# A two-layer graph network on one core: layer 0 gathers its raw input, with the dense stage begun beside its last nine quads

## The reference

```
# layer 0
qk, v  = x @ Wqk + bqk, x @ Wv + bv
score  = clip(sum(qk[dst] * qk[src], -1) / sqrt(128), -5, 5)
attn   = segment_softmax(score, dst)
h      = segment_sum(attn * v[src], dst) @ Wo + bo + x
x      = layernorm(x + gamma * norm(h) + beta)
# layer 1, 8 heads of 16
n      = norm(x) * ln1_w
xl, xr = n @ lin_l_w.T + lin_l_b, n @ lin_r_w.T + lin_r_b
z      = leaky_relu(xl[src] + xr[dst] + edge_attr @ lin_edge_w.T, 0.2)
alpha  = segment_softmax(sum_per_head(z * att), dst)
y      = x + segment_sum(alpha * xl[src], dst) + attn_bias
y      = y + relu(norm(y) * ln2_w @ fc_w.T) @ proj_w.T
x      = layernorm(x + y)
```

## Time and profile before

| | before |
|---|---|
| median of 3 runs | 3092.32 us (3090.11 to 3101.77) |
| profiled execution | 3122.75 us |
| its span | 3120.9 us |
| mean granted clock of TensorE | 0.862 |
| PE, PEld busy | 2211.6 (71%), 1775.4 us (57%) |
| DVE, ACT, POOL busy | 1709.5 (55%), 652.8 (21%), 1767.4 us (57%) |
| DMA | 413.24 MB, mean 132 GB/s |

### The profile page before, as it was taken

How to read it: one execution, slowest core, us unless ns; L and a number is a source line. 1 busy time by engine, 2 the same in 40 slices (tenths; PEclk the granted TensorE clock), 3 DMA queues, 4 the chain that set the end, 5 groups by cost and what they waited for, 6 DMA issues and landing times. The chain is left out here.

```text
span 3120.9 us, 55922 instructions
## 1 busy us (share of the span) xinstructions
PE 2211.6 (71%) x15187; PEld 1775.4 (57%) x15187; DVE 1709.5 (55%) x7262; ACT 652.8 (21%) x1876; POOL 1767.4 (57%) x1751
## 2 busy tenths in 40 slices
PE   4666666666666666656378777777777777788879
PEld 3666666666666666644255555555555555565656
DVE  4444444444444444478245555555655566565766
ACT  0222222222222222235021111111111111111123
POOL 2666666666666666644656555555555565555312
PEclk8988888888888888877688888888998999988869
DMA  6555555555555555513454444444444444444301
GB/s 212 158 150 148 152 151 150 149 151 151 149 149 151 151 151 149 139 44 88 141 163 130 121 137 133 123 130 138 137 134 120 132 139 137 137 124 130 92 15 38
DMA packets 392325, 413.24 MB, mean 132 GB/s; under 512 B 61167, under 2 KB 336367, under 8 KB 385360
## 3 DMA queue, kind: packets, MB, share of 16 engines
q1 hardware_dynamic: 304992, 233.79, 25.4%
q0 software_dynamic: 66560, 163.68, 19.3%
q10 hardware_dynamic: 20592, 13.63, 1.4%
HBM read 393.41 MB, written 17.47 MB: 132 GB/s over the span
## 5 line engine op out<-in xcount | busy, mean ns | idle before, releaser
L832 POOL DMA_INDIRECT rows<-xl_tab,src_cols x832 | 848.1, 1019 | 592.8 <-DVE message L974 356.4
L260 POOL DMA_INDIRECT rows<-qkv_tab,src_cols x832 | 819.7, 985 | 501.8 <-remote 250.1
L307 PE MATMUL tile_sums<-gather,rows 128*128 128x128 f32 x1664 | 401.6, 329 | 413.8 <-issue 396.8
L339 DVE CUSTOM_DVE_ANT_0 product<-rows,q_dst 128x128 f32<-128x128 f32 x832 | 233.7, 281 | 654.3 <-remote 641.5
L307 PEld LDWEIGHTS tile_sums<-gather,rows 128*128 128x128 f32 x1664 | 307.0, 230 | 460.7 <-issue 454.0
L996 DVE SCALAR_TENSOR_TENSOR node_sums<-node_sums,shrunk,tile_sums 128x128 f32 x832 | 280.7, 337 | 316.5 <-remote 294.6
L309 PE MATMUL tile_sums<-gather,ones 128*128 128x128 f32 x1664 | 380.8, 316 | 0.0
L883 PEld LDWEIGHTS z_ps<-spread,window 128*128 128x128 f32 x1664 | 253.3, 220 | 203.9 <-issue 101.8
L930 PE MATMUL tile_sums<-onehot,message 128*128 128x128 f32 x1664 | 304.3, 323 | 79.9 <-issue 72.0
L348 DVE TENSOR_TENSOR node_sums<-node_sums,tile_sums 128x256 f32 x832 | 350.8, 422 | 4.7 <-PE tile_sums L309 1.6
L930 PEld LDWEIGHTS tile_sums<-onehot,message 128*128 128x128 f32 x1664 | 245.3, 218 | 143.6 <-issue 129.9
(11 more groups left out here) (153 smaller groups left out, 2532.8 us busy)
## 6 DMA issues: line engine op xcount, KB each, us to landing
window<-qkv_tab SPq DMA_DIRECT2D x832, 64.0 KB
attr<-in_attrT SPq DMA_DIRECT2D x52, 1024.0 KB
window<-xr_tab SPq DMA_DIRECT2D x832, 64.0 KB
rel_bc<-rel_rows SPq DMA_DIRECT2D x208, 128.0 KB
rel_bc<-rel_rows SPq DMA_DIRECT2D x52, 512.0 KB
rows<-qkv_tab,src_cols POOLq DMA_INDIRECT x832
rows<-xl_tab,src_cols POOLq DMA_INDIRECT x832
qkv_tab<-qkv ACTq DMA_DIRECT2D x13, 512.0 KB, 4.9
```

Of the source, the lines that this page charges most:

```text
L260: nc.gpsimd.indirect_dma_start(out=rows[:, q * QT + i, :], out_offset=None, in_=qkv_tab, in_offset=bass.IndirectOffsetOnAxis(ap=src_cols[: ...
L307: nc.tensor.matmul(bank[:, i % 2, 0, :], rows[:, q * QT + i, P:], gather1[:, q % 2, i, :], start=True, stop=True)
L832: nc.gpsimd.indirect_dma_start(out=rows[:, r, i, :], out_offset=None, in_=xl_tab, in_offset=bass.IndirectOffsetOnAxis(ap=src_cols[:, tile: ...
```

## The change

Blocks (a) to (d) become one block, with all quads written out (no hardware loop), and its steps run from T = 0 to 217, with no barrier between layer 0 and the dense stage.

- The score of an edge is x[src] . (M x[dst] + m) + (m' x[dst] + c) up to scale, with M = Wqk Wqk^T. PE makes M and the vectors at the start from transposed weights, and from them a table `p_tab` of 129 columns per node (the last is the constant). The gathers read the input x itself (512 B a row), and wait only for `src_cols`, which is now loaded first. Four blocks of `p_tab` are made ahead and one in each of steps 0 to 8; SP's windows (129 wide) of quad Q < 13 wait for a stored block. Wv Wo is one matrix `w_vo`, applied in the dense stage.
- The weighted one-hot is not a transpose any more: ACT makes |column - rel| (`measure`, four Abs to bf16), the exponential and its negative, and Relu(weight - weight |column - rel|) (`weigh`, four). PE has 8 spread records a quad, in halves that wait for `scored` of the quad before, and 16 of `add_up`, one step later than before. DVE's sums are two quads behind as before. `node_sums` is cleared by block.
- The dense block b starts at step T = 199 + b: projection, residual and moments at T, root, shift and norm 0 at T+1, POOL's `add_parts` (three operations), moments 1 at T+4, root 1 and the transposes at T+5, tables at T+6, scaled by the reciprocal root, with centred weights `w_cen`, so that no norm of x1 is made there. POOL puts `add_parts` of blocks 0 to 3 behind the gathers of quads 204 to 207. Only four buffers of x (`x_nm`) are loaded, the first four 16 quads ahead.
- Layer 1: `AHEAD` is 4. The biases of lin_l and lin_r are the bias operands of ACT's two halves of z, roots and shifts for all x1 are made at the start, and ACT normalises x1 (`norm_x1`, four operations) at quads 9 to 21. Some semaphores are merged. The MLP block loads `lin_l_b` and adds it on POOL to the attention bias.

```diff
-    qkv_tab = nc.dram_tensor("qkv_tab", (NP, 2 * P), F32).ap()
+    p_tab = nc.dram_tensor("p_tab", (NP, P + 1), F32).ap()
+    AHEAD0 = 4
+    DENSE = 199
+    EARLY = 4
...
+        steps = max(quads + 2, DENSE + blocks + 6)
...
+                pool.wait_ge(src_in, DMA)
+                for Q in range(quads):
+                    r = Q % AHEAD0
+                    if Q >= AHEAD0:
+                        pool.wait_ge(summed, 2 * (Q - AHEAD0 + 1))
+                    for i in range(QT):
+                        tile = Q * QT + i
+                        nc.gpsimd.indirect_dma_start(
+                            out=rows[:, r, i, :], out_offset=None, in_=t["x"],
...
+                    if Q == quads - EARLY:
+                        pool.wait_ge(lr_loaded, 5 * DMA)
+                        pool.wait_ge(w_scaled, 1)
+                    if Q >= quads - EARLY:
+                        add_parts(Q - quads + EARLY)
+                for b in range(EARLY, blocks):
+                    add_parts(b)
...
+                for T in range(steps):
+                    for k in range(2):
+                        if T + 1 < quads:
+                            spread_p(T + 1, k)
+                        if 0 <= T - 1 < quads:
+                            add_up(T - 1, k)
+                    if T + QUADS < node_groups:
+                        make_p(T + QUADS)
+                    b = T - DENSE
...
+                    if 0 <= b < blocks:
+                        project(b)
...
+                    if 0 <= b - 6 < blocks:
+                        tables(b - 6)
+                    if 0 <= b - 5 < blocks:
+                        turn_y(b - 5)
...
+                for T in range(steps):
+                    if T < quads:
+                        measure(T)
...
+                    if 0 <= b - 1 < blocks:
+                        root0(b - 1)
+                    if 0 <= b - 5 < blocks:
+                        root1(b - 5)
+                    if T < quads:
+                        weigh(T)
+                    if 0 <= b - 1 < blocks:
+                        norm0(b - 1)
+                    if 0 <= b - 6 < blocks:
+                        keep_tables(b - 6)
+                    if 0 <= b - 5 < blocks:
+                        keep_hT(b - 5)
...
-    AHEAD = 8
+    AHEAD = 4
```

More of the change, by code:

```diff
@@ new lines, in build @@
+        xlr = sb("xlr", [P, 2, QT, 2 * P])
+        share = sb("share", [P, QT])
+        stats = sb("stats", [P, 2, QT, 6])
+        mv0 = sb("mv0", [P, 2, QT, 2])
+        std = sb("std", [P, 2, 2, QT])
+        rstd = sb("rstd", [P, 2, 2, QT])
+        shift = sb("shift", [P, 2, 2, QT])
+        p_dst = [ps(f"p_dst{i}", [P, 2, 2 * P]) for i in range(2)]
+        tile_sums = [ps(f"tile_sums{i}", [P, 2, 2, P]) for i in range(2)]
+        o_ps = ps("o_ps", [P, QT, P])
+        t_ps = ps("t_ps", [P, QT, P])
@@ new lines, in build @@
+        lr_loaded = sem("l01_weights_in")
+        w_flipped = sem("w_flipped")
+        w_kept = sem("w_kept")
+        m_made = sem("m_made")
+        m_kept = sem("m_kept")
+        x_in = [sem(f"xT_in{i}") for i in range(2)]
+        p_made = sem("p_made")
+        p_kept = sem("p_kept")
+        p_stored = [sem(f"p_stored{i}") for i in range(2)]
+        cleared = sem("cleared")
+        gathered = [sem(f"gathered{i}") for i in range(AHEAD0)]
+        window_in = [sem(f"window_in{i}") for i in range(SLOTS)]
@@ new lines, in build @@
+        x_nm_in = [sem(f"x_nm_in{i}") for i in range(QT)]
+        projected = sem("projected")
+        inverted = sem("inverted")
+        h_made = sem("h_made")
+        stats_made = sem("stats_made")
+        mv0_made = sem("mv0_made")
+        std0_made = sem("std0_made")
+        rstd0_made = sem("rstd0_made")
+        shift0_made = sem("shift0_made")
+        u_made = sem("u_made")
+        scaled = sem("u_scaled")
+        x_shifted = sem("x_shifted")
+        y_made = sem("y_made")
+        stats1_made = sem("stats1_made")
@@ L112, in _, with load_x @@
             def _(sp):
[L113 to L117, removed]
+                def load_x(b):
+                    n = block_tiles(b)
+                    sp.dma_start(x_nm[:, b % QT, 0:n], x_dram[b, :, 0:n]).then_inc(x_nm_in[b % QT], DMA)
@@ L126, in _ @@
+                for b in range(QT, blocks):
+                    sp.wait_ge(h_made, b - QT + 1)
+                    sp.wait_ge(x_shifted, b - QT + 1)
+                    load_x(b)
+                sp.wait_ge(tiles_stored, 4 * DMA)
+                for i in range(2):
+                    sp.wait_ge(tables_stored[i], 2 * ((blocks + 1 - i) // 2) * DMA)
             @block.gpsimd
@@ new lines, in score @@
+                def score(Q, k):
+                    dve.wait_ge(p_spread, 2 * Q + k + 1)
+                    if k == 0:
+                        dve.wait_ge(gathered[Q % AHEAD0], (Q // AHEAD0 + 1) * QT * DMA)
+                        if Q >= 2:
+                            dve.wait_ge(clip_done, Q - 1)
+                    for i in range(2):
+                        o = nc.vector.tensor_tensor_reduce(product[:, 2 * k + i, :], rows[:, Q % AHEAD0, 2 * k + i, :],
+                                                           p_dst[k][:, i, 0:P], 1.0, p_dst[k][:, i, P:P + 1], ALU.mult,
+                                                           ALU.add, scores[:, Q % 2, 2 * k + i:2 * k + i + 1])
+                    o.then_inc(scored, 1)
@@ L682, in build @@
     ROWS = 16
-    AHEAD = 8
-    SLOTS = 4
-    quads = tiles // QT
+    AHEAD = 4
     node_sums = attention.enter_context(nc.sbuf_tensor("node_sums1", [P, NP], F32))
@@ L869, in _ @@
                         raise_falls(s)
+                    if Q >= LAG and Q - LAG < blocks:
+                        norm_x1(Q - LAG)
             @block.tensor
```

1035 lines of the change are left out of this document (502 added, 533 removed).

## The result

The changed kernel took 2989.53 us, the median of 4 runs (2972.82 to 2993.63), beside 3093.3 for the kernel before: ratio 0.965, with the 95% interval 0.961 to 0.969. That is 104 us less where 192 were forecast, inside the whole range and 30 us above the main case's own (2840 to 2960). Its profiled execution took 2993.63 us with a span of 2991.8, against 2931 in the sum of the forecast.

A forecast was written before the change was run, and what follows sets the result against it. No engine is full; runs of N gathers were taken to hold back PE's reports about 1.40 N + 0.4 us. Terms -35 - 8 - 63 - 27 - 60 + 1 = -192 gave 2931 profiled, 2900 as median; range 2670 to 3005.

The forecast's parts named there:

- main case: Whole kernel: all terms as summed, 2900 us, own range 2840 to 2960; chance 0.45.
- A, front: Before the first product: gathers read x and start early, first product at 35 us; -35 (-20 to -45).
- B, loop of layer 0: 208 quads of layer 0: cadence stays 6.1 us, halves scored earlier; -8 (bounds +10 and -202).
- C, dense stage: Dense stage begun beside quads 199 to 207, ACT setting these steps: 144 us instead of 207; -63 (-10 to -95).
- D, start of layer 1: Start of layer 1: 16 gathers instead of 40 before the first gate; -27 us (-10 to -34).
- E, loop of layer 1: 198 quads of layer 1: z_ready replaces message as POOL's gate; -60 us taken (-176 to +200).
- F: MLP: one more load and one POOL addition; +1 us.
- R2: Layer 1 stays at 6.99 us a quad, paced by PE's own chain; E at nothing, 2960 us; chance 0.18.
- R4: Layer 1 in lockstep at 8.0 us a quad: +200 in place of -60, 3160 us; chance 0.08.
- R3: Dense stage: overlap brings nearly nothing, steps in series, held PE answers late; C at -10, 2953 us; chance 0.08.
- R1: Layer 0 paced by POOL at 5.1 us a quad: -202 in place of -8, 2706 us; chance 0.17.

The follow-up runs named there:

- the ring of 19: Kernel before with a ring of 19 quads of rows instead of 16 in layer 1, AHEAD still 8: 2990.81 us beside 3096.28, ratio 0.9662.
- the third set: Set of runs in which the kernel before took 2559.09 us; the changed kernel with AHEAD 8 and 19 ring quads instead of 16 took 2555.60, ratio 0.9986.

## Why the prediction was right or wrong

The time lies inside the range, 15 us below its upper end, and faster was forecast. It is outside the main case's own range, and the gain is about half of what I gave: the total is held by layer 1, which gave more than I took, against layer 0 and the dense stage, which gave 79 us less.

- **A, front**: -35 forecast, -28.6 measured (70.05 to 41.47). The size is near, the reason was another: after 16 gathers (to 25.3) PE still made blocks of p until 40.2, and only then the first `p_dst`. I had put the hold of the gathers there.
- **B, loop of layer 0**: -8 forecast. The steady part is that: 1117.7 to 1109.8 for 186 quads. What failed is the sentence that nine blocks of p beside a pacing POOL cost nothing: the first 13 quads took 50 us more. I counted PE's records and not where ACT's copy stood in its queue, ahead of the exponential that releases the next quad. Moving it gave 34 us of that back.
- **C, dense stage**: -63 forecast, -12 measured (207.2 to 195.0). I said ACT would set the steps at 8 to 12 us, table loads among it; the eight steps from quad 199 to 207 come to 72 us in my sum and took 104.5, 13.1 each. ACT's table loads were not the reason, and DVE's wait for the projection was the larger part: late in its step, with the next quad's scores queued behind it. The rest I had at 72 (60 and the step of quad 207), and it took 90.5.
- **D, start of layer 1**: -27 forecast. This step rests on a misread row. ACT's record at 1546.77 is not the first z behind a run of 40 gathers but the third; the first was read at 1512.00, 22.0 us after the first gather, as it is now (23.5, 1469.41 to 1492.91). That the 23 us of the forecast came is luck: PE had waited for the attributes, finished z at 1492.81, and ACT read it 0.1 us later.

```profile
1489.02 2.04 PE L899 MATMUL z_ps<-attr,w_e 128*128 128x512 f32 x2 [8.42 <-DMA attr<-in_attrT]
```

  What did come earlier is the third z, 35.1 us after the first gather instead of 56.8. By the ring of 19, which keeps the long start, that is worth some 5 us.
- **E, loop of layer 1**: -60 taken, of up to -176. D and E together were forecast at -87 and gave -104.7 (1439.8 to 1335.1), nearly all of it E. The mechanism was right, as the ring of 19 shows; the size was low. That ACT's biases cost nothing was wrong by a little: its half of z takes 0.69 us (L851) where it took 0.60 (L843).
- **F**: +1, and the part behind the last gather took 187.3 us instead of 191.1.

The sum of the measured parts: A -28.6; quads 0 to 199 1233.0 instead of 1212.2, +20.8; C -12.8; layer 1 -104.7; rest -3.8: -129, the difference of the two profiled executions (3122.75 to 2993.63). Here C is taken from the profile of the kernel before (207.8). On the scale of medians it is 104.

Of the rivals, R2 (layer 1 unchanged) and R4 (lockstep at 8.0) didn't happen. R3 (the overlap brings nearly nothing) did, for one half of its reason, engines in series; whether a held PE answers late there was not tested. Its chance was 0.08. R1 (layer 0 at POOL's pitch, 5.1) didn't happen in the result, but it did in the third set, for the changed kernel, at 5.05.

The reading under all of this, that N gathers in a row hold back what PE reports for 1.40 N + 0.4 us, is not borne out as a rule. The pace with four gathers is right (6.0). With 16 a product of DVE at 70.05 reads what PE has just made, in the middle of the run; with 40 the first z is read after 22.0 us, the second after 46.7. In the kernel before with the ring of 19, under the same 40 gathers without a gap (1468.08 to 1518.46), ACT reads the second z at 1506.68, before they end. What stands is that gathers pace both layers and that some of PE's reports, and PE's own records, are late while they run. The pace doesn't depend on the bytes of a row (5.97 with 512 B against 6.01 with 1 KB).

## What to carry to other kernels

Ask of each wait of the engine that paces which of its conditions comes last, and remove that one before rebuilding anything: here one number, or three more slots in a ring, gave about all that 1,560 lines of diff gave. When work is put into a running pipeline, write down for each in-order engine what stands behind the new wait; a copy ahead of an exponential and a residual ahead of a score cost some 34 and 16 us without any engine being full. Follow one value by its own records, first, second and third, before a late record is read as the end of a wait. And time such a change in more than one session before its gain is booked.

## What the runs showed of the hardware

- While POOL issued gathers, some of what PE had finished reached other engines late: in layer 1 of the kernel before the second z 22.8 us late, the first 0.3. In the trace of the third set both were read within 0.1 us, 19 and 21 gathers into a run. The kernel before took 3086 to 3096 us (medians) in the one condition and 2559 in the other. What sets the condition is open. So is the mechanism: PE's records stretch in the same runs (18.4 us for a z that takes 2.5), so that it may be PE itself that is slowed, its reports, or both.
- One gather of 128 rows took 0.95 us and they start 1.26 apart, with 1 KB or 512 B a row. The third set shows what that sets: 5.05 us per four.
- With half of the gathers gone the granted clock of layer 0 rose from 0.88 to 1.00, of its two levels 1.2 and 2.4 GHz the higher throughout, with PE busy 88% instead of 67% of the time.
- In the step of quad 201 a one-hot of DVE that takes 0.48 us took 3.12 (1309.43) while POOL ran its additions on SBUF (from 1309.77 on). That the two are cause and effect no run here tests:

```profile
1309.43 3.12 DVE L533 TENSOR_SCALAR spread<-rel_bc,iota_col 128x512 f32<-128x512 bf16 x1
...
1309.77 1.27 POOL L266 TENSOR_TENSOR x<-x_nm,beta_o 128x512 f32<-128x512 f32 x1
...
1310.99 1.26 POOL L269 TENSOR_TENSOR u<-u,gamma 128x512 f32<-128x512 f32 x1
```
